# First attention layer on one core: scores of a round and the next round's first chunk in one TensorE group, turned a slot earlier

## The reference

```
q = einsum('qdh,bcd->bhcq', Q, xn) * sq      # 16 heads of 64; k and v alike
att = einsum('bhcq,bhCq->bhcC', q, k) / 64   # 512 x 512 scores of a head
att = where(causal, att, -inf)
p = softmax(att);  y = einsum('bhcC,bhCv->bhcv', p, v)
z = einsum('dvh,bhcv->bcd', W, y) * ...
```

## Time and profile before

| what | value |
|---|---|
| time, median of 3 runs (lowest, highest) | 1213.15 us (1212.77, 1213.98) |
| span of the profiled execution | 1209.2 us |
| TensorE busy | 1189.8 us (98%), 8908 matmuls |
| VectorE, ScalarE, GpSimd busy | 990.7 us (82%), 819.7 us (68%), 409.9 us (34%) |
| chain that ended last | 82% TensorE, 10% VectorE, 4% ScalarE |
| granted TensorE clock | 1.000 of 2.4 GHz over the span |

### The profile page before, as it was taken

How to read it: one execution, slowest core, us unless ns; L and a number is a source line. 1 busy time by engine, 2 the same in 40 slices (tenths; PEclk the granted TensorE clock), 3 DMA queues, 4 the chain that set the end, 5 groups by cost and what they waited for, 6 DMA issues and landing times.

```text
span 1209.2 us, 23949 instructions
## 1 busy us (share of the span) xinstructions
PE 1189.8 (98%) x8908; PEld 887.1 (73%) x8908; DVE 990.7 (82%) x1918; ACT 819.7 (68%) x2174; POOL 409.9 (34%) x364
## 2 busy tenths in 40 slices
PE   8999999999999999999999999999999999999998
PEld 6777677767776777677767776777677767767766
DVE  6888588968886889688968896888788878988886
ACT  6785577567756775677567756775677768767875
POOL 2216420640064006400640064006400658535820
PEclk9999999999999999999999999999999999999999
DMA  7004300410041004200420042004200420000000
GB/s 258 1 30 134 97 1 21 132 61 2 20 134 62 1 19 134 62 1 19 135 62 1 20 134 62 1 17 136 62 1 16 138 62 2 7 12 19 1 11 27
DMA packets 44292, 63.93 MB, mean 53 GB/s; under 512 B 8144, under 2 KB 18384, under 8 KB 43920
## 3 DMA queue, kind: packets, MB, share of 16 engines
q1 hardware_dynamic: 44176, 62.39, 16.6%
HBM read 59.48 MB, written 2.88 MB: 52 GB/s over the span
## 4 chain that ended last, share of the span: by engine, by line
PE 82%; DVE 10%; ACT 4%; issue 2%; DMA 1%; SPq 1%; POOL 0%; DVEq 0%; ACTq 0%; POOLq 0%
PE psum L1435 14%; PE psum L1483 14%; PE psum L1505 12%; PE psum L64 9%; PE psum L66 9%; PE psum L65 9%; PE psum L1542 5%; DVE mneg L1123 2%; ACT probs L754 2%; PE psum L1444 2%; PE psum L1718 1%; DVE sg L1173 1%; PE psum L1509 1%; PE psum L1781 1%; DVE sg L1163 1%
## 5 line engine op out<-in xcount | busy, mean ns | idle before, releaser
L754 ACT ACTIVATE probs<-psum,mneg 128x512 f32<-128x512 f32 (+3 forms) x640 | 329.7, 529 | 127.1 <-DVE mneg L1123 122.5
L1123 DVE TENSOR_REDUCE mneg<-psum 128x2 f32<-128x1024 f32 (+2 forms) x320 | 253.6, 820 | 99.9 <-PE psum L1444 99.5
L1114 DVE COPY pt<-psum 128x512 f32<-128x512 f32 x320 | 205.2, 682 | 29.7 <-PE psum L1483 27.9
L1483 PE MATMUL psum<-ident,probs 128*128 128x128 f32 x1600 | 223.3, 278 | 6.1 <-DVE pt L1114 2.1
L1483 PEld LDWEIGHTS psum<-ident,probs 128*128 128x128 f32 x1600 | 176.5, 140 | 37.9 <-issue 19.5
L561 POOL TENSOR_TENSOR qk_lo<-sg,qk_hi 128x512 fp32r<-128x512 f32 x64 | 92.7, 1455 | 162.0 <-ACT qk_hi L798 162.0
L525 POOL TENSOR_TENSOR rstd<-var,mhalf 128x4 f32<-128x4 f32 x7 | 7.1, 1012 | 399.8 <-DVE var L1009 399.8
L1505 PE MATMUL psum<-pt,v_all 128*64 128x384 f32 (+5 forms) x1088 | 142.6, 412 | 0.0
L754 ACT ACTIVATION_READ_ACCUMULATOR probs<-psum,mneg 128x1 f32 x640 | 131.8, 206 | 0.0
L1435 PE MATMUL psum<-qk_hi 64*128 64x512 f32 (+7 forms) x640 | 121.6, 375 | 2.2 <-ACT probs L754 1.9
L1505 PEld LDWEIGHTS psum<-pt,v_all 128*64 128x64 f32 (+1 forms) x1088 | 69.5, 135 | 66.2 <-issue 50.7
(11 more groups left out here) (275 smaller groups left out, 2422.4 us busy)
## 6 DMA issues: line engine op xcount, KB each, us to landing
crow<-weights SPq DMA_DIRECT2D x256, 128.0 KB, 3.0
rrow<-sums SPq DMA_DIRECT2D x128, 128.0 KB, 3.0
gu_raw<-in_gu SPq DMA_DIRECT2D x1, 2176.0 KB, 11.5
x_all<-in_x SPq DMA_DIRECT2D x8, 256.0 KB, 6.4
out_rows<-x_all SPq DMA_DIRECT2D x7, 256.0 KB, 2.3
down_raw<-in_down SPq DMA_DIRECT2D x1, 1088.0 KB, 13.7
wqkv_raw<-in_wqkv SPq DMA_DIRECT2D x1, 896.0 KB, 6.8
wqkv_raw<-in_wqkv SPq DMA_DIRECT2D x1, 512.0 KB, 5.0
```

The source lines that it names most:

```text
L754: last = act.activation(probs[:, h * HALF + PROB[t]:h * HALF + PROB[t] + w], bank[score_bank(rnd, c) + h][:, o:o + w], ACT.Exp, bias=mneg[ ...
L1114: dve.tensor_copy(turned_rows(rnd)[:, s % 2, :, 3 - s // 2, :], turn_bank(rnd, s).rearrange("p (j q) -> p j q", q=P)).then_inc(pt_ready, 1)
L1123: last = dve.tensor_reduce(mneg_h[:, :, t], psum[:, b:b + 2, o:o + P * (t + 1)], AX, ALU.max, negate=True)
L1483: last = nc.tensor.transpose(turn_bank(rnd, s)[:, i * P:(i + 1) * P], probs[:, v:v + P], ident[:, :])
```

## The change

On TensorE, slot `n` now begins with one group of scores: chunk 1 of round `n`, its masks first and its products after them, then the products of chunk 2, then those of **chunk 0 of round `n+1`**, then the masks of both. Behind the group round `n-1` is weighed. Then round `n` is turned in steps 0, 1, 2, then q and k of round `n+2` are projected, then steps 3 and 4 follow. Each chunk has banks of its own (0 and 1, 2 and 3, 4 and 5), and the steps are turned into banks 7, 2, 3, 5, 4. ScalarE and VectorE are put into the matching order. Where a slot waited for the rest of k of its own round, the group now waits, ahead of chunk 2, for the rest of k of the next one. The core of the diff (the second layer keeps its banks and counts through `n < ROUNDS0` cases that are left out here):

```diff
-SCORE_BANK = [0, 2, 0]
+SCORE_BANK = [0, 2, 4]
+        TURN_BANK0 = [7, 2, 3, 5, 4]
+        TURN_BANK0_FIRST = [6, 2, 3, 5, 4]
...
@@ ScalarE, first_layer, for p in range(PAIRS) @@
                     if p == 0:
                         exps(n, 0)
-                    if p < PAIRS - 1:
-                        round_q(n + 1, SCALE0)
-                    if p:
-                        take_tile1(n - 1)
-                        exps(n, 0)
-                    if p < PAIRS - 1:
-                        round_k(n + 1)
-                    else:
-                        copy_combt(b)
-                    if p == 0:
-                        exps(n, 1)
-                    exps(n, 2)
-                    if p == 0 and b:
-                        copy_acc(b - 1)
+                        round_q(n + 1, SCALE0)
+                        round_k(n + 1)
+                    exps(n, 1)
+                    exps(n, 2)
+                    if p:
+                        copy_y(n - 1)
+                    elif b:
+                        copy_acc(b - 1)
+                    if p < PAIRS - 1:
+                        next_exps(n + 1, 0)
+                        next_exps(n + 1, 1)
+                    if p < PAIRS - 2:
+                        round_q(n + 2, SCALE0)
+                        round_k(n + 2)
+                    if p == PAIRS - 2:
+                        copy_combt(b)
+                    take_tile1(n)
...
@@ VectorE, first_layer, for p in range(PAIRS) @@
                     if p == 0:
                         row_maxima(n, 0)
-                        row_maxima(n, 1)
                         rest_q(n + 1, SCALE0)
                         rest_k(n + 1)
...
+                    row_maxima(n, 1)
+                    row_maxima(n, 2)
+                    if p < PAIRS - 1:
+                        row_maxima(n + 1, 0)
                     route(b, p)
+                    take_turned(n, range(3))
+                    invert_sums(n)
+                    if p < PAIRS - 2:
+                        rest_q(n + 2, SCALE0)
+                    if p < PAIRS - 1:
+                        take_turned(n, [3])
+                    elif b:
+                        add_rows(b - 1)
+                    if p < PAIRS - 2:
+                        rest_k(n + 2)
...
@@ TensorE @@
+            def score_group(n):
+                p = n % PAIRS
+                if p:
+                    pe.wait_ge(pt_ready, (n - 1) * (TURNS - 1) + 3)
+                score_masks(n, 1, True)
+                score_products(n, 1, n % 2, ROWS0, True).then_inc(scored, 1)
+                if p:
+                    pe.wait_ge(pt_ready, n * (TURNS - 1))
+                    pe.wait_ge(pt4_ready, n)
+                if p < PAIRS - 1:
+                    pe.wait_ge(qk_lo_ready, (n + 1) * 2 + 2)
+                score_products(n, 2, n % 2, ROWS0)
+                if p < PAIRS - 1:
+                    pe.wait_ge(exp_done, exp_count(n, 0))
+                    score_products(n + 1, 0, (n + 1) % 2, ROWS0)
+                score_masks(n, 2).then_inc(scored, 1)
+                if p < PAIRS - 1:
+                    score_masks(n + 1, 0).then_inc(scored, 1)
...
+                if p == 0:
+                    first_head(b)
+                score_group(n)
+                if p == PAIRS - 1:
+                    pe.wait_ge(combt_ready, b + 1)
+                if p:
+                    weigh_pair(n - 1)
+                elif b:
+                    project_out(b - 1, 3).then_inc(acc_done, 1)
+                for s in range(3):
+                    turn_step0(n, s)
...
+                    project_qk(n + 2, [0])
+                    pe.wait_ge(pt_ready, n * (TURNS - 1) + 1)
+                    project_qk(n + 2, [1])
+                elif p == PAIRS - 2:
+                    pe.wait_ge(y_ready, n)
+                    turn_weights(b)
+                elif b:
+                    pe.wait_ge(y_ready, n)
+                    turn_acc(b - 1)
+                if p < PAIRS - 1:
+                    turn_step0(n, 3)
+                    turn_step0(n, 4)
```

More of the change, by code:

```diff
@@ L242, in rows_bank @@
             return bank[6] if b < B - 1 else bank[7]
+        WEIGHTS_BANK = bank[6]
         UNIT_BANKS = [bank[0:2], bank[2:4]]
         def qk_banks(n):
-            if n < ROUNDS0 and n % PAIRS < 2:
-                return (bank[4], bank[5]) if n % PAIRS == 0 else (bank[6], bank[5])
+            if n < ROUNDS0 and n % PAIRS < 3:
+                return [(bank[4], bank[5]), (bank[6], bank[5]), (bank[7], bank[6])][n % PAIRS]
             return bank[6], bank[7]
@@ L756, in exps, with next_exps @@
                 last.then_inc(exp_done, 1)
+            def next_exps(rnd, h):
+                act.wait_ge(max_ready, max_count(rnd, 0))
+                act.wait_ge(turned, turn_count(rnd - 1, h))
+                t = CHUNKS[0][0]
+                o, s = h * HALF + PROB[t], slice(h * TILES + t, h * TILES + t + 1)
+                last = act.activation(probs[:, o:o + T], bank[score_bank(rnd, 0) + h], ACT.Exp, bias=mneg[:, s], accum_out=rsum[:, rnd % 2, s])
+                if h:
+                    last.then_inc(exp_done, 1)
             def take_values(b, fills):
@@ L1434, in score_products, with score_masks @@
                         for h, r in enumerate(head_rows):
-                            mm(bank[score_bank(rnd, c) + h][:, o:o + w], ql[r, 0, qs_], kl[r, 1, ks], start=i == 0 and n == 0, stop=False, **K)
-            def score_masks(rnd, c):
+                            ins = mm(bank[score_bank(rnd, c) + h][:, o:o + w], ql[r, 0, qs_], kl[r, 1, ks], start=i == 0 and n == 0 and not masked, stop=masked, **K)
+                return ins
+            def score_masks(rnd, c, first=False):
                 n = len(CHUNKS[c])
@@ L1444, in score_masks @@
                         last = mm(blocks[:, :, piece * DQ:(piece + 1) * DQ], later0[r, piece, :], hide0[r, :].unsqueeze(1).to_broadcast([DQ, n, DQ]),
-                                  start=False, stop=True, **K)
-                last.then_inc(scored, 1)
+                                  start=first and piece == 0, stop=not first, **K)
+                return last
             def score_chunk(rnd, c, buf, head_rows):
                 score_products(rnd, c, buf, head_rows)
-                score_masks(rnd, c)
+                score_masks(rnd, c).then_inc(scored, 1)
             def score_rest(rnd, buf, head_rows):
@@ L1585, in turn_weights, with turn_step0, slot @@
                 pe.wait_ge(comb_ready, b + 1)
-                nc.tensor.transpose(bank[7][:, 0:P], rexp[:, :, :].rearrange("p t e -> p (t e)"), ident[:, :]).then_inc(combt_done, 1)
+                nc.tensor.transpose(WEIGHTS_BANK[:, 0:P], rexp[:, :, :].rearrange("p t e -> p (t e)"), ident[:, :]).then_inc(combt_done, 1)
             def score0(n, c):
                 score_chunk(n, c, n % 2, ROWS0)
-            def first_chunks(b):
-                n = b * PAIRS
-                pe.wait_ge(qk_lo_ready, n * 2 + 2)
-                if b:
-                    pe.wait_ge(su_done, b * UNITS)
-                score0(n, 0)
-            def slot(n, head):
+            def turn_step0(n, s):
+                pe.wait_ge(exp_done, exp_count(n, [0, 1, 1, 2, 2][s]))
+                turn_blocks(n, s)
+            def score_group(n):
[16 more added lines that the diff above has]
+                    score_masks(n + 1, 0).then_inc(scored, 1)
+            def slot(n):
                 p = n % PAIRS
@@ L1641, in first_head @@
                     unit_down(b - 1, UNITS - 1)
-                first_chunks(b)
-                score0(b * PAIRS, 1)
+                pe.wait_ge(qk_lo_ready, n * 2 + 2)
+                if b:
+                    pe.wait_ge(su_done, b * UNITS)
+                score0(n, 0)
+                pe.wait_ge(v_taken, (b + 1) * FILLS)
+                project_qk(n + 1, range(2))
                 if b:
                     project_out(b - 1, 2)
-                pe.wait_ge(v_taken, (b + 1) * FILLS)
-                project_qk(b * PAIRS + 1, range(2))
-                pe.wait_ge(exp_done, exp_count(b * PAIRS, 0))
-                score0(b * PAIRS, 2)
-                if b:
-                    project_out(b - 1, 3).then_inc(acc_done, 1)
             def units(b):
                 n = (b + 1) * PAIRS - 1
-                turn_step(n, 0)
-                turn_step(n, 1)
-                pe.wait_ge(exp_done, exp_count(n, 2))
                 half_unit(b, 0, 0)
-                turn_step(n, 4)
+                turn_step0(n, 3)
                 half_unit(b, 0, 1).then_inc(gu_done, 1)
-                turn_step(n, 3)
-                turn_step(n, 2)
+                turn_step0(n, 4)
+                pe.wait_ge(pt_ready, n * (TURNS - 1) + 3)
                 project_unit(b, 1)
+                if b:
+                    pe.wait_ge(x1_ready, b)
                 pe.wait_ge(y_ready, n)
@@ L1705, in _ @@
                 for p in range(PAIRS):
-                    slot(b * PAIRS + p, lambda: first_head(b))
```

(1 more changed line is left out.)

79 lines of the change are left out of this document (22 added, 57 removed).

## The result

The changed kernel takes 1217.12 us (median; 1215.57 to 1218.12), the kernel before beside it 1212.77 (1211.31 to 1213.98): a ratio of 1.0038, 95% interval 1.0025 to 1.0050. It is slower by some 4.5 us. The forecast was 1214 us, no change; the time lies in the range of 1205 to 1222, above the 2.4 us that the forecast called no change, and falls under rival 2, a wait in each slot.

The account below looks back on a forecast made before the run. The prediction took TensorE's own program, without waits in steady slots, as the bound. Seven batches at -0.8 us and the first at +0.9 gave +0.1 on 1209.2, the median offset and longer hand-overs 1214 us; range 1205 to 1222.

Parts of the forecast that it names:

- no change: Whole kernel: time within 2.4 us of 1213.15, forecast at 1214 us; chance 0.35.
- rival 2: Steady slots: chain through ScalarE longer than laid, TensorE waits each slot for rest of k; 7 us, 1220 us; chance 0.30.
- What the grouping removes: TensorE: one spell of scores fewer in seven slots a batch, 0.36 us each, 2.52 us a batch.
- 1193 us: Whole kernel: the time with all 56 spells removed, worth 20.2 us, and no wait at all.
- The steady slot: Work of 8.40 us; chunk 2 waits 0.22 for the rest of k in every other slot, 0.44 a batch.
- Theory B: Steady slot, follow-up rival: the queue of ScalarE or VectorE alone sets the time; no chance given.
- The hand-over: Between engines: a signal takes 0.03 to 0.06 us; TensorE hears of the rest of k at 9.58 after 9.52.
- The ends of a batch: Slots 0, 1, 7 and feed-forward part: losses of 0.34 and 0.10, 0.33, 0.28 and 0.71, 0.2 us a batch.
- feed-forward seam: Feed-forward part: later step 4 and `silu` push VectorE's gates; bounds 0 and 0.5 us, 0.2 taken.
- The sum: Whole kernel: 2.40 lost against 2.52 gained a batch, -0.8 us for seven; first batch +0.9; total +0.1.
- In the steady slots TensorE waits for nobody: TensorE before the change: one steady slot of 8.75 us shows no wait, so only closer instructions shorten it.
- The offset: Whole kernel before: profiled span 1209.2 us stands some 4 us below the median of 1213.15; the difference carries over.

Follow-up runs that it names:

- first run: Changed kernel with TensorE's wait for the rests of q and k moved behind chunk 2 from each batch's second slot on (the late wait): 1201.18 us, ratio 0.9918.
- the run in which that queue came nearer and nothing changed: Changed kernel with chunk 1's masks put back behind its products: 1216.91 us, ratio 1.0044.
- the last run: Changed kernel with the three waits ahead of chunk 2 reordered, the one for the rests of q and k written first: 1212.9 us, ratio 1.0012.
- the last two runs: Changed kernel with VectorE's rest of k ahead of its copy of step 3, 1215.70 us; changed kernel with the rests' wait written first of three, 1212.9 us.
- the fastest version: Changed kernel with the wait for the rests moved behind chunk 2 and slot 7's `turn_acc` behind the feed-forward part's first half unit: 1197.73 us, ratio 0.9887.
- the one with the wait of 2.58: The fastest version, with chunk 1's maxima ahead of the rests of q and k on VectorE in the first batch's first slot: 1198.90 us, ratio 0.989.

## Where the forecast was right and where it was wrong

The range held; "no change" did not, and the reason for it failed in the steady slot. That 1214 us came as near as it did is in part luck, since errors of both signs lie in the sum (5, below).

1. **What the grouping removes: right, the size slightly low.** TensorE's busy time fell, nothing in the group starts bare, and a slot without waits is 0.40 us shorter than before (first run), where the sum had 0.36. The Trainium skill (TensorEngine Tiling (Array Packing), Key Properties) says that a change of the tiling mode drains TensorE. The trace agrees in so far as such a change costs time: 0.34 us for one way out and in. By that alone 1193 us had been worked out; the version without the two avoidable waits takes 1197.7.
2. **The steady slot: the step that failed.** It was: "A wait of 0.22 pushes TensorE back, so that the next slot has none: the loss is 0.22 in every other slot." The idle time was read rightly and the conclusion drawn from it was wrong. The chain was laid from ScalarE's queue (7.04) alone; the other thing that the rounding of q waits for, the q projection, does not stand in it. By the forecast's own numbers its end is at 5.97 + 0.94 = 6.91 (184.29 to 184.83, and 0.40 for the last matmul), the earlier one as long as nothing is pushed. With the wait of 0.22 ahead of it, it ends at 7.13 and takes the lead (measured 187.20 - 180.07 = 7.13). From then on TensorE's push moves the chain too, and the next slot waits as long. The run with chunk 1's masks behind its products and the one with the rest of k ahead of the copy bear this out (what lies outside the loop changes nothing, the order within it neither), and the late wait removes it. Theory B, a queue alone, falls by the start of the rounding, 0.15 behind where ScalarE's queue would have it, and by the run in which that queue came nearer and nothing changed. Five slots lose 8.63 - 8.35 = 0.28 each, 1.4 a batch and not 0.44.
3. **The hand-over: 0.147 and not 0.06.** With 0.06 the loop would be 8.54 and still longer than 8.35, as the last run shows (8.53); two thirds of the loss stay without it.
4. **The ends of a batch: in kind right, in size mixed.** Slot 7's `turn_acc` lost 0.52, not 0.71. Chunk 2 in slots 0 and 1 of the later batches comes 0.39 late in both (0.34 and 0.33 laid out). The group of slot 7 waits 0.19 (0.28). The first batch waits 1.96 and 1.14 (2.1 and 1.3). The feed-forward seam of batches 1 to 6 grew by 0.20 on average, the value taken, but by 1.4 after the first batch, with a wait of 1.17 at 97.70 us for VectorE's gate (L1184, whose tile lies in `probs`), which nothing in the forecast had.
5. **The sum.** The first batch, from its first chunk to the next one's, lost 0.5 us (forecast 0.9), and each later one 0.57 (forecast a gain of 0.12). The first figure is near by luck: the five steady distances won 1.6 us more than in a later batch, since the slots before were 9.06 to 9.52 there and not 8.75, and the feed-forward seam lost the 1.4. "In the steady slots TensorE waits for nobody" was read from one slot of one batch. The error of 0.69 a batch, 4.8 us in all, is the steady slots' 0.9, less 0.3 for the grouping and 0.2 for `turn_acc`; some 0.3 is left, of which slots 0 and 1 are 0.1 and the rest stays open.
6. **The offset.** "Some 4 us" between the profiled span and the median joined two different things: the time of an execution is 1.7 to 1.9 us over its span in every run that has both (1215.57 and 1213.8 for the changed kernel), so that the profiled execution of before, with its span of 1209.2, took about 1211 by estimate, some 2 below its median. Part of that is the clock: of the runs of the kernel before beside the experiments, the 15 with a mean granted clock of 1.0 have a median of 1210.69 us, the 18 with 0.999 one of 1212.76. The profiled executions of both kernels were at 1.000, and the 4.6 us between their spans agree with the medians. That decided nothing.

Rival 2 named the outcome, a wait in each slot, but by another mechanism than the one found: not a chain that is longer by itself but one that its own wait lengthens.

## What to carry over

When a wait is laid out over a repeating slot, follow the chain round until it meets its own start, and compare the length of that loop with the slot's work; if the loop is the longer one, the loss recurs in every slot. Ask of each chain not only what bounds it now but what is second: 0.13 us behind stood the thing that took over. A wait belongs directly ahead of the first instruction that needs it: here chunk 2 didn't need the rests of q and k, and 0.4 us of work between made 16 us. And one steady slot is not all of them: compare the distance in each batch before a sum is built on one.

## What the runs showed of the hardware

- TensorE starts 0.055 us behind the end of a VectorE instruction if one semaphore is awaited, or if the last of three to come is the one written first; it starts 0.147 behind it if that one is written last (the changed kernel, and the last two runs). Two further waits would then cost 0.046 each; that the waits are gone through from the last written to the first would fit the three cases, and no run looks at it in another way.
- Such a start 0.147 late has no bracket in the steady slot: the wait of 0.23 there is seen only in the distance of two rows.
- One transpose costs 0.11 us among its like and 0.45 between score matmuls of 64 rows.
- The granted clock fell to 0.50 for 3.4 us behind the first slot's wait in the profiled execution of the fastest version (wait 1.94) and for 6.8 us in the one with the wait of 2.58; in those of the changed kernel and of the first run, with a wait of 1.96 at the same place, it stayed at 1.00. So the wait alone does not settle it.
